# A ViT layer on one core: three of the second image's patch tiles are embedded between the two halves of the first image's attention, and the norm there is split

## The reference, cut to what matters

```
h = patches @ Wp + bp + pos                    # tokenizer, per image 1024 x 256
a = layernorm(h);  n = layernorm(a) * gamma + beta
q, k, v = n @ W_qkv.T                          # 8 heads of 32
gate = sigmoid(a @ W_gate.T + b_gate)
attn = softmax(q k^T / sqrt(32));  out = (attn^T v) * gate
h = h + a + out @ W_final.T + b_final
h = h + ffn(layernorm(h))                      # gelu hidden of 1024, router, one of 8 experts per token
```

## Time and profile before

| | |
|---|---|
| median of 3 runs | 1770.38 us (1767.6 to 1772.08) |
| the profiled execution: its own time | 1784.43 us |
| its span, first to last instruction | 1782.6 us |
| mean granted TensorE clock | 0.966 of full |
| PE busy | 1617.7 us, 91% |
| DVE busy | 1186.9 us, 67% |
| ACT busy | 941.7 us, 53% |
| POOL busy | 368.2 us, 21% |
| share of PE in the chain that ended last | 72% |

### The profile page before, as it was taken

How to read it: one execution, slowest core, us unless ns; L and a number is a source line. 1 busy time by engine, 2 the same in 40 slices (tenths; PEclk the granted TensorE clock), 3 DMA queues, 4 the chain that set the end, 5 groups by cost and what they waited for, 6 DMA issues and landing times.

```text
span 1782.6 us, 29438 instructions
## 1 busy us (share of the span) xinstructions
PE 1617.7 (91%) x10934; PEld 1107.2 (62%) x10934; DVE 1186.9 (67%) x2070; ACT 941.7 (53%) x1564; POOL 368.2 (21%) x290
## 2 busy tenths in 40 slices
PE   8796999989999999899999989998978774999998
PEld 6463566555655564566456646664535353999998
DVE  2377677858686878577767776777665644555555
ACT  0464756655574657465746575657564651222222
POOL 0202000210021011202110210021000192555554
PEclk9898999999999999999999999999998896999999
DMA  4313134322523152416141604170419436566664
GB/s 170 89 54 71 28 104 114 87 58 82 127 67 86 63 137 48 113 49 139 33 113 54 153 15 113 54 165 2 95 41 217 86 83 162 183 207 209 209 205 144
DMA packets 131014, 188.57 MB, mean 106 GB/s; under 512 B 21606, under 2 KB 95980, under 8 KB 130620
## 3 DMA queue, kind: packets, MB, share of 16 engines
q1 hardware_dynamic: 112588, 121.57, 29.2%
q0 software_dynamic: 17856, 63.80, 11.2%
q10 hardware_dynamic: 432, 1.31, 0.2%
HBM read 85.55 MB, written 51.68 MB: 77 GB/s over the span
## 4 chain that ended last, share of the span: by engine, by line
PE 72%; DVE 11%; issue 8%; ACT 4%; DMA 3%; SPq 1%; POOL 1%; another core or an unknown queue 0%; POOLq 0%; ACTq 0%; DVEq 0%
PE ps L572 13%; PE ps L823 12%; PE ps L586 11%; PE ps L539 8%; DVE nmax L1248 6%; PE ps L560 3%; PE ps L811 3%; PE ps L623 3%; PE ps L645 3%; PE ps L599 3%; PE ps L606 2%; PE ps L647 2%; PE ps L646 2%; ACT pr L949 2%; DMA token_rows<-staged_b 2%
## 5 line engine op out<-in xcount | busy, mean ns | idle before, releaser
L1248 DVE TENSOR_REDUCE nmax<-ps 128x1 f32<-128x1024 f32 x512 | 623.8, 1221 | 238.6 <-PE ps L572 221.2
L949 ACT ACTIVATE pr<-ps,nmax 128x1024 f32<-128x1024 f32 x512 | 570.5, 1114 | 318.6 <-DVE nmax L1248 281.3
L572 PE MATMUL ps<-st 96*128 96x512 f32 x1024 | 406.5, 482 | 74.2 <-ACT pr L949 63.6
L572 PEld LDWEIGHTS ps<-st 96*128 96x128 f32 x1024 | 171.1, 195 | 273.5 <-ACT pr L949 127.9
L586 PE MATMUL ps<-pr,vs 128*32 128x256 f32 x4096 | 277.3, 391 | 25.1 <-DVE vs L1047 18.1
L823 PE MATMUL ps<-wd_high,hg 128*128 x1136 | 222.7, 289 | 0.0
L586 PEld LDWEIGHTS ps<-pr,vs 128*32 128x32 f32 x4096 | 110.1, 110 | 171.1 <-issue 81.7
L977 ACT ACTIVATE hg<-ps 128x512 fp32r<-128x512 f32 x142 | 77.7, 596 | 210.2 <-PE ps L811 208.5
L823 PEld LDWEIGHTS ps<-wd_high,hg 128*128 128x128 f32 x1136 | 182.8, 192 | 0.0
L539 PE MATMUL ps<-wp,xt 128*128 128x256 f32 x672 | 172.9, 379 | 0.0
L823 PE MATMUL ps<-wd_low,hg 128*128 x568 | 161.2, 284 | 0.0
(11 more groups left out here) (153 smaller groups left out, 1935.9 us busy)
## 6 DMA issues: line engine op xcount, KB each, us to landing
st<-qk SPq DMA_DIRECT2D x192, 256.0 KB, 5.1
xt<-x_in SPq DMA_DIRECT2D x58, 384.0 KB, 3.1
token_rows<-staged_b SPq DMA_DIRECT2D x64, 256.0 KB, 4.9
token_rows<-staged_a SPq DMA_DIRECT2D x64, 256.0 KB
token_rows<-hres POOLq DMA_DIRECT2D x8, 1024.0 KB, 5.3
wd_low<-w_down SPq DMA_DIRECT2D x64, 128.0 KB, 4.1
pr<-x_in SPq DMA_DIRECT2D x6, 384.0 KB, 10.0
rows<-token_rows,slot_from POOLq DMA_INDIRECT x71
```

The costliest lines, as they stand in the source:

```text
L572: last = mm(ps[:, 2 * (k % SR) + j, :], stq[:, hh, i * P:(i + 1) * P], stk[:, hh, j * 512:(j + 1) * 512], start=True, stop=True)
L949: actv(pr[:, k % PR, :], ps[:, 2 * (k % SR):2 * (k % SR) + 2, :].rearrange("p a n -> p (a n)"), ACT.Exp, bias=nmax[:, k % 16:k % 16 + 1], ...
L1248: V.reduce_max(nmax[:, k % 16:k % 16 + 1], ps[:, 2 * (k % SR):2 * (k % SR) + 2, :].rearrange("p a n -> p (a n)"), AX_X, negate=True).then_ ...
```

## The change: what it does

For image 0 alone (that is, for the front of image 1):

- `EMBED_0` takes the place of `EMBED_AT`: the 15 parts of tiles 0 to 4 lie at steps 8, 9, 11, 12, 14, then 16, 17, 19, 20, 22, then 24, 25, 27, 28, 30. Nine of the 24 steps have none.
- Tiles 5, 6 and 7 are embedded in the block between the halves, ahead of PE's wait for `emb_h` and of `weigh` 7.
- Tiles 6 and 7 are read from `staged_a` (as `x_second`), where SP's queue loads them right behind tiles 0 and 1, with a semaphore of their own. The counts of `x_in` that later images wait for are 16 lower.
- DVE's `norm_between` takes the place of `norm_1`, `norm_2` and `gated` in the block: statistics of tiles 0 to 4, then position and statistics of tiles 5 to 7 as they come, the aggregation, `gated`, and the normalisation into `n`. The normalisation into `a` comes later, behind the maximum of step 33.

```diff
+        x_second = staged_a[:].rearrange("p a k d -> p (a k d)")[:, 0:2 * KC * P].rearrange("p (t k n) -> p t k n", t=2, k=KC)
...
+        EMBED_0 = {8 + 8 * m // 5: divmod(m, 3) for m in range(15)}
...
             def load_rest(b):
-                for t in range(2, TILES):
+                if b == 1:
+                    for t in range(2):
+                        sp.dma_start(x_second[:, t], x[b, TILES - 2 + t]).then_inc(S["x_second"], 16)
+                for t in range(2, TILES if b > 1 else TILES - 2):
                     hold(sp, "emb_mm", b * TILES + t - 1)
                     load_tile(b, t)
...
             def embed(b, t, part):
 
+                source = xt[:, t % 2] if b > 1 or t < TILES - 2 else x_second[:, t % 2]
                 if part == 0:
-                    wait(pe, x_in[t % 2], b * 64 - 32 + 16 * (t // 2))
+                    if b == 1 and t >= TILES - 2:
+                        wait(pe, "x_second", 32)
+                    else:
+                        wait(pe, x_in[t % 2], b * 64 - 32 + 16 * (t // 2) - 16 * (b > 1))
...
                     if k == G_STEPS:
 
+                        if not before:
+                            for t in range(5, TILES):
+                                for part in range(3):
+                                    embed(b + 1, t, part)
                         if after:
                             wait(pe, "emb_h", (b + 1) * TILES + TILES)
...
+            def norm_between(b, par):
+
+                for t in range(5):
+                    wait(dve, "emb_h", b * TILES + t + 1)
+                    V.bn_stats(bst[:, 0, t, :], hres[par][:, t, :])
+                for t in range(5, TILES):
+                    embedded(b, par, t)
+                    wait(dve, "emb_h", b * TILES + t + 1)
+                    last = V.bn_stats(bst[:, 0, t, :], hres[par][:, t, :])
+                last.then_inc(S["stats1"], 1)
+                aggregate(b, 1)
+                gated(b - 1, 0)
+                normalise(n, hres[par], b, 2, "n_ready")
...
                         scale_v(b, 7)
                         if before:
                             low_norm(b - 1)
-                        if after:
+                        if not before:
+                            norm_between(b + 1, 1 - par)
+                        elif after:
                             norm_1(b + 1, 1 - par)
...
+                    if not before and k == G_STEPS + 1:
+                        normalise(a, hres[1 - par], b + 1, 1, "a_ready")
```

More of the change, by code:

```diff
@@ L192, in vit_layer_kernel @@
         S = {}
-        for name in ("consts early setup pos_in0 pos_in1 x_first0 x_first1 x_first2 wp_in pos_mm pos_relu pos_mm2 pos_sum pos_done x_in0 x_in1 emb_mm emb_h "
+        for name in ("consts early setup pos_in0 pos_in1 x_first0 x_first1 x_first2 x_second wp_in pos_mm pos_relu pos_mm2 pos_sum pos_done x_in0 x_in1 emb_mm emb_h "
                      "stats1 stats3 var1 var3 eps1 eps3 rstd1 rstd3 pow_ready "
@@ L538, in embed @@
                 for k in range(2 * part, 2 * part + 2):
-                    last = mm(spare(t)[:, 0:D], xt[:, t % 2, k, :], wp[:, k, :], start=(k == 0), stop=(k == KC - 1))
+                    last = mm(spare(t)[:, 0:D], source[:, k, :], wp[:, k, :], start=(k == 0), stop=(k == KC - 1))
                 if part == 2:
@@ L749, in image @@
                         project(b, 1, j, c)
-                    if after and k in EMBED_AT:
-                        t, part = EMBED_AT[k]
+                    spread = EMBED_AT if before else EMBED_0
+                    if after and k in spread:
+                        t, part = spread[k]
                         if t < 2 and part == 0:
@@ L1240, in image @@
                             keep_logits(b - 1, 0)
-                        if after:
+                        if before and after:
                             norm_2(b + 1, 1 - par, before)
-                        gated(b, 0)
+                        if before:
+                            gated(b, 0)
                         if before:
@@ L1263, in image @@
                         low(b, 1, LOW1_AT[k])
-                    if after and k in EMBED_AT and EMBED_AT[k][1] == 2:
-                        embedded(b + 1, 1 - par, EMBED_AT[k][0])
+                    spread = EMBED_AT if before else EMBED_0
+                    if after and k in spread and spread[k][1] == 2:
+                        embedded(b + 1, 1 - par, spread[k][0])
                     if after and k in LOW0_AT:
```

## The result

| | before | the change |
|---|---|---|
| median of 20 runs, measured together | 1768.37 us (1765.24 to 1773.79) | 1772.57 us (1764.54 to 1783.69) |
| ratio, with its 95% interval | | 1.0024 [1.0013, 1.0035] |
| the profiled execution: its own time, span | 1784.43, 1782.6 us | 1764.54, 1762.6 us |

The change is slower by 4.2 us, 0.24%, and its interval is clear of 1. Forecast was 2.0 us faster. The times are also wider spread than those of before, and the profiled execution is the fastest of the twenty. So this one profile can't show the loss. It shows what the change does when all goes well.

The account below looks back on a forecast made before the run. PE was taken to bound image 0's steps 8 to 31, DVE and POOL the block between its halves. -3.5 + 1.5 = -2.0 us, median 1770.38 to 1768.4 us; range for 8 in 10: 1764.2 to 1773.5.

Parts of the forecast that it names:

- First half: Steps 8 to 31 of image 0: nine embedding parts leave PE, 3.5 us earlier at the 32nd score's end.
- Rival 2: Steps 8 to 31: PE stays the bound, first half gains 0; +1.5 us, 1771.9 us; chance 0.08.
- The block up to maximum 32: Block between image 0's halves: maximum 32 starts 16.8 us after the 32nd score (S) against 16.3, +0.5 us.
- Rival 3: Block's 36 embedding instructions run at half clock, 0.44 us each; +6.0 us, 1776.4 us; chance 0.05.
- `a` behind maximum 33: After the block: `a` holds DVE, so score 36 comes later, at S+24.3 against S+22.6; taken as +1.5 us.
- The sum: Whole kernel: -3.5 + 1.5 = -2.0 us, so the median goes from 1770.38 to 1768.4 us.
- The step that failed: POOL's sum with `a`, after the block: starts at S+21.7 instead of S+15.1, costs nothing.
- rival 1: PE after the block: the pause beside `a` prolongs the half clock; +2.6 us, sum +0.6, 1771.0 us; chance 0.15.

Follow-up runs that it names:

- timed_sums: The change, with POOL's first sum of image 1 held until `vs` 8 is done and the second until `vs` 9 is; 1.0003 of before, +1.0 us.
- norm_only: Before, with only DVE's new order in image 0's block (`gated` early, `a` behind maximum 33) and the old embedding; 1.0016 of before, +3.4 us.
- after_filler: The change, with seven idle products on PE behind score 33 of image 0; 1.0027 of before, +6.7 us.
- before_late_sum: Before, with POOL's sums for image 1 made to wait for the maximum of step 36; 1.0011 of before, +1.7 us.
- after_early_a: The change, with `a` moved back to right behind `n`, ahead of the maxima; 0.9994 of before, -0.5 us.
- before_early_gated: Before, with `gated` of image 0 moved ahead of the norm, inside POOL's wait; 0.9996 of before, -0.2 us.
- embed_only: The change's embedding move with DVE's old order in the block (`n`, `a`, `gated`, then the maxima); 1.0012 of before, +1.8 us.
- spread_pieces: The change, with one tile of `a` behind each of maxima 33 to 40 and POOL's sums of image 1 in pieces; 0.9995 of before, -0.2 us.
- after_nosum: The change, with POOL's two sums for image 1 left out but for 8 columns of one tile; 1.0003 of before, +0.4 us.
- spread_timed: The change, `a` spread over steps 33 to 40, POOL's sums held for `vs` 9 and 10; 0.9992 and 0.9997 of before in two sessions.
- after_pieces: The change, with POOL's two sums of image 1 cut into 8 pieces each; 1.0012 of before, +1.6 us.

## Why the prediction was wrong

**Where the time went.** The edits' own gain is there in the good case. The loss is a collision that the good case just misses. The two kinds of execution are 7.1 us apart in their stretches (88.94 against 81.81): 3.0 us is what a late clock costs in timed_sums, and 4.1 us are left for `vs` held behind POOL's second sum (22.64 against timed_sums' 18.55). This parting is an estimate, since the clock of the held execution was back some 2 us earlier than that of timed_sums and then fell a second time behind the hold. Shown are the hold (in the change, norm_only, after_filler, before_late_sum, after_early_a and before_early_gated, the length of `vs` each time what was left of the sum) and its price in a profile. Shown, too, is that the change's loss goes when the sums do, or when they are held back. Not shown is that all of it is the hold: embed_only is slower by 1.8 us without one. That most timed runs fall into the held case is inferred from their times: the three profiled executions with the good case, at 1764.54, 1763.66 and 1763.31 us, rank first, second and first among the 20, 12 and 12 of their sets, the one with the held case sixth of 12. With -2.1 and +5.0 us for the two, a rise of 4 would take six executions in seven in the held one; three profiles in four were in the good one. That part doesn't fit well, and stays open. So does whether being profiled has a part in it, or being first: every profile of these sessions is of the first execution of its set. Nor do two cases 7.1 us apart explain sets of the change that are 13.0 to 19.2 us wide (before's own are 7.6 to 16.4), and part of the loss goes with the mean clock, as said above.

**Term by term.**

- *First half, -3.5.* Measured -2.8 (43.79 to 40.97), inside the bounds of -4.4 and -1.6. PE is busy 38.54 of 40.81 us in it now, so some parts that overflow their idle time did stay. Rival 2 is wrong.
- *The block up to maximum 32, +0.5.* S+16.7 against S+16.3, +0.4: right. The two added DMAs and the wait for `xt` cost nothing. Rival 3 is wrong: the block's products took 0.222 us each.
- *`a` behind maximum 33.* Score 36 at S+24.1, forecast S+24.3. The whole block, score 31 to 36, +1.4, forecast +1.5: right.
- *The sum, -2.0.* -2.1 in the good case's stretch. Whether the time of the kernel would have followed is not shown: spread_pieces has -2.2 in its stretch and no long hold, and timed it is 0.2 us faster than before.
- *The step that failed:* "POOL's sum with `a` starts at S+21.7 instead of S+15.1; only `added` at the end of image 0's steps waits for it, far behind: nothing." The time was right (S+21.7), and who waits for its result too. What I didn't ask is what runs beside it while it lasts: 9.2 us of POOL from S+21.7 to S+30.9 lie over DVE's `vs` 8 at about S+26, which the second sum stretches from 0.29 to 4.30 us where it gets in first. Before, the sums ended 0.85 us ahead of it. So the term put at nothing is worth about 4 us in such an execution, against a forecast gain of 2.0.
- *The clock, and rival 1 (+2.6, 0.15).* "the later rest could hold the array at half clock for longer" came true in size, 3.0 us, in those executions in which the clock comes back late. My sum with it gives +0.6 to +0.9, and after_nosum and timed_sums stand there (+0.9). Missing was that it moves `vs` 8 by half a microsecond, into the second sum.

On the first, the Trainium skill ("SBUF — State Buffer", section "Who interferes with whom") says that a VectorE instruction with two SBUF inputs contends with a GpSimd instruction that reads SBUF. Its section "SBUF: two separate sides" says that whichever starts first gets the shared pair of ports for its whole instruction, while the other fully blocks. The trace agrees: `vs` was held to 0.14 to 0.16 us behind the sum's end. It is the rule that I should have weighed, with POOL's rows of 4.5 us with two SBUF inputs. On the second, the rule of the Trainium skill that the prediction gives ("TensorE: Matmul & The Clock Gate", Part 1) fits: one program had its clock back before score 36 in one execution and after it in another. The traces show that the return moves, by over 4 us, and not what moves it.

**Is there a better version?** By its two profiles' stretches (81.2 and 81.3 us) spread_timed is faster than before by 2.8 and 2.6 us. Timed, that doesn't arrive: 0.9992 and 0.9997, with 1 inside both intervals. It is better than the change (medians 3.4 us apart in the same session, 0.9997 beside 1.0023), and no kernel here is shown to be faster than before. Why these 2.6 to 2.8 us don't show is open.

## What to carry to other kernels

When an instruction is moved, follow what it releases as well: ask of the released work not only who waits for its result but what it will run beside. A GpSimd sum of several microseconds like the one here (4.5 us, two SBUF inputs) wants a place where DVE has no short instruction with two SBUF inputs on the critical path; a wait on that instruction's own semaphore puts it there, at no cost that shows here (1.0003 and 0.9992). And where the timed spread widens while the profile looks well, take the profile again, until it falls on a run as slow as the median.

## What of the hardware was not expected

- DVE's `vs` of 128x128, 0.29 us alone, took 4.31, 4.30, 4.30, 1.71, 0.48 and 0.47 us when it started while a sum ran on POOL, always until 0.14 to 0.16 us after its end. At the seam of two sums back to back, 0.08 us wide, one that started 0.06 us ahead of the first sum's end took 0.29 us, three times in three. With POOL's sums in pieces of 128x256 the longest were 0.52 us (after_pieces) and 0.83 us (spread_pieces).
- The clock can be back over 4 us later in one execution than in another of the same program, after the same rest. From 162 on it was 1.00 in the good case; in the held case, which lies 1.0 us later, it was still 0.50 from 166 to 167, and 0.90 from 167 to 168. Keeping PE busy in the rest (after_filler) only moved the dip behind it. A stall of 2.5 us of PE behind a held `vs` was followed by a second dip, 0.50 from 171 to 177.
